# Five rearrangements in a two-layer token model on one core: row-max split inside its pass, early region padding, a new order at the gate's end, ranks and projection moved, embedding by batches

## The chip, the cores and the metric

One core of a Trainium2 chip runs the whole program. Five engines work beside each other, each on its own list of instructions: PE (TensorE, matrix products), DVE (VectorE), ACT (ScalarE), POOL (GpSimd) and SP (SyncE, which only issues DMAs). They meet through semaphores. The metric is the device time of one execution in microseconds (us), the median of several.

## The reference

4096 tokens (8 sequences of 512, width 192) pass five blocks, each added to the stream `h`:

```python
tok = wte[input_ids]                                   # gathered rows
Q, V = ln(tok) @ W_proj.T, tok @ W_val.T               # 8 heads of 64
trace = 0.99 * trace0 + 0.1 * einsum('bhip,bhiq->hpq', Q[:, :, :-2], V[:, :, 2:]) / denom
h  = shifted(Q) @ trace, heads joined, @ W_out.T       # L0 token block
h += linear_attention(layernorm(h))                    # 12 heads of 16, 44 features
h += soft_moe(layernorm(h))                            # 64 experts
h += attention_with_fake_quant(layernorm(h))           # 12 heads, 8 bits
x  = h_norm + attention(layer_norm(h_norm))            # full softmax, float32 accuracy
h += x + moe_mlp(layer_norm(x))                        # top 2 of 8 experts, hidden 768
```

In the last line each token goes to its two best experts by `xn @ gate_w`, and the two results are added with softmax weights.

## The kernel before

The program is six stages, each one or more blocks; all engines meet at a block's end. A batch is one sequence: 128 partitions by T = 4 tokens by 192. `Fori` is a loop on the engine itself; a Python loop is written out. `Link` makes DVE wait for its own last instruction; `Signal` is a semaphore that is counted per batch.

**Embedding, `embed_and_trace` (0 to 146 us).** POOL gathers the token rows by 32 indirect DMAs (line 246), four a batch, and waits for batch b-1 to land before it issues batch b+1. DVE and PE wait for all seven weight loads first. DVE computes the statistics of four batches together (`stats(half)`, L266, L151 to L156, L273) and then in a loop normalises each (`rows(b, j)`: four L279, L283, L284). PE (`products`) shifts rows (L361), turns them (L368) and adds their products with later rows (L375); ACT copies (L327, L331). After the last batch come small products one after the other: L388, L395, L400, then L406 (8 heads of 64 rows), and then h itself (L419), for which ACT first copies each batch of QT to a staging tile QTs (L348).

**Quantised attention, `quantised_attention`.** Its first pass over the scores (PE L1651, DVE L1661, ACT L1685) is a loop over batches. SP's part of it only spreads the queries of a batch over partitions (L1636, 4 DMAs), when the batch two before is done.

**Routed attention, `routed_attention` (from 1598 us).** A preparing block loads weights, and on POOL sets `Wp` to 0 (L2006), the ones of `V` (L2007) and the ones rows of the two key stacks (L2010); DVE waits for all. Pass 1 computes all scores in bf16 parts (PE L2202) and DVE keeps each row's maximum in `MX` (L2072); between score units, PE makes the queries, keys and values of batch b+2. The next block is pass 2. It begins by splitting `MX` into three bf16 parts on DVE (L2426, L2428), turning them (PE L2283), copying them (DVE L2431, ACT L2397), and placing them into rows of the query stack by DMA (L2251, `shift_rows`), so that the product gives score minus maximum. Then for each batch there are 12 steps n: PE makes the next two score pairs (L2296), ACT takes their exp (L2410), PE multiplies by values (L2360). PE runs ahead by one step. In the steps of batch b it also works for earlier ones: at n = 1 `ranks(b - 2)` (L2331, L2333), then `project(b - 1)` half 0 (L2309), at n = 3 half 1, at n = 8, 9, 11 the turned rows (L2315) and gate logits (L2323) of b-1. DVE divides the output (L2511 to L2517, result `OT`), finds the best two experts (`best_two`, to L2480), prepares the next residual rows (L2499, L2501), adds the projection (L2442; in `add_projection` preceded by `places`, L2486 to L2494), takes statistics and normalises (L2459). POOL computes rstd (L2558), scales (L2562, L2565) and sends the rows to their experts' regions in `routed_in` by indirect DMA (`send`, L2574), two sends of 4 DMAs a batch; the second waits until the first has landed, because both read one buffer whose return index is rewritten between them.

After the last batch DVE works out which tile belongs to which expert (up to `m.TID`, L2547), and SP then pads each expert's region behind its last row (L2269, 8 DMAs of 196 KB at places read from a table) and loads the first four experts' weights (L2593, 1252 KB each).

**Routed experts, `routed_experts`.** The block loads row tiles (SP L2620, L2621), after the pads have landed, turns them (PE L2654) and runs 39 tiles of two products (L2664, L2668, L2679). A last block adds the returned rows.

Of the kernel before, what the change touches and what calls it, by code (L numbers as in the profile page):

```python
# [9 lines left out]
BF16 = mybir.dt.bfloat16  # L10
# [148 lines left out]
def setup(nc, m, io):  # L159
# [19 lines left out]
    m.zero_filled = nc.alloc_semaphore("zero_filled")  # L179


def embed_and_trace(nc, m, io):
# [8 lines left out]
    QTs = [e(DC, [NC, T, P + 1]) for _ in range(2)]  # L191
    w = Cut(m.arena, R_AT + 4 * SLOT, E_AT)
    WpT, WvT = w(DC, [NC, TH * TD]), w(DC, [NC, TH * TD])
    WoT, Wp = w(TD, [TH, D]), w(TD, [TH, D])
    tr0, trT = w(TD, [TH, TD]), w(TD, [TH, TD])
    YT, U = w(DC, [NC, TH * TD]), w(TD, [TH, D])
# [6 lines left out]
    s_idx, s_w, s_const, s_rows, s_tok = sem("idx_loaded"), sem("tok_weights_loaded"), sem("constants_set"), \  # L203
        [nc.alloc_semaphore(f"rows_gathered{b}") for b in range(B)], sem("tok_ready")
# [7 lines left out]
    s_lk, s_qs, s_h, s_hc, s_l3, s_sk = (sem(n) for n in (  # L212
        "embed_chain", "q_staged", "h_product", "h_stored", "embed_chain3", "embed_stats_chain"))
    NH2 = B * T // 2

    with nc.Block(no_gpsimd_drain=True) as block:
        @block.sync
        def _(sp):
            sp.dma_start(idx, io.x.rearrange("b (p t) -> p b t", t=T)).then_inc(s_idx, 16)
            for dst, src in ((lnw, io.tok_ln_w.partition_broadcast(P)), (lnb, io.tok_ln_b.partition_broadcast(P)),  # L220
                             (WpT, io.tok_WpT.rearrange("(c p) n -> p c n", c=NC)),
                             (WvT, io.tok_WvT.rearrange("(c p) n -> p c n", c=NC)),
                             (WoT, io.tok_WoT.rearrange("(h p) n -> p h n", h=TH)),
                             (Wp, io.tok_W_proj.rearrange("(h p) n -> p h n", h=TH)),
                             (tr0, io.tok_trace0T.rearrange("h q p -> q h p"))):
                sp.dma_start(dst, src).then_inc(s_w, 16)

        @block.gpsimd
        def _(pool):
# [14 lines left out]
            for b in range(B):  # L244
# [7 lines left out]
            pool.wait_ge(s_rows[B - 1], 16 * T)  # L252
            pool.sem_inc(s_tok, 1)

        @block.vector
        def _(v):
            v.memset(QT[:, :, :, :, 0], 0.0)
            v.wait_ge(s_w, 16 * 7)

            def stats(half):  # L260

                link = Link(v, s_sk, 8 * half)
                for b in range(B // 2 * half, B // 2 * (half + 1)):
                    v.wait_ge(s_tok, b + 1)
                    for t in range(T):
                        ins = v.bn_stats(m.ST[:, b, t, :], tok[:, b, t, :])  # L266
                link(ins)
                part = lambda a: a.rearrange("p b t -> p (b t)")[:, NH2 * half:NH2 * (half + 1)]
                ln_constants(v, link, m.ST.rearrange("p b t k -> p (b t) k")[:, NH2 * half:NH2 * (half + 1), :],
                             part(m.wk[0]), part(m.wk[1]), part(m.mean), part(m.var))  # L270
                v.sem_inc(s_v, 1)
                v.wait_ge(s_std, half + 1)
                link(v.reciprocal(part(m.rstd), part(m.wk[2])))  # L273

            def rows(b, j):

                v.wait_ge(s_tsfree, b + 1)
# [17 lines left out]
            v.tensor_copy(YT, ps[0:DC, 0:2, :]).then_inc(s_yc, 1)  # L295
            v.tensor_scalar(tr0, tr0, 0.99, None, ALU.mult).then_inc(s_l3, 1)
# [6 lines left out]
            v.tensor_copy(U.rearrange("p (k h) n -> p k h n", k=4),  # L303
                          ps[0:TD, 4:8, 0:2 * D].rearrange("p k (h n) -> p k h n", h=2)).then_inc(s_gc, 1)
# [14 lines left out]
        def _(act):  # L319
# [3 lines left out]
            def part(b, j):  # L323
# [10 lines left out]
            for half in range(2):  # L334
# [2506 lines left out]
```

## Time and profile before

| | us |
|---|---|
| median of 3 runs | 2666.76 (2664.4 to 2668.61) |
| the profiled execution | 2661.37 |
| its span, first to last instruction | 2659.7 |
| busy in it: PE, DVE, ACT, POOL | 1947.6, 1493.0, 1065.1, 395.2 |

The span is what the rows below count from. Busy time of an engine says little alone: the stages follow each other and have different limits. Rows of the timeline give start, duration, engine, source line, operation, written tile, read tile, shape and count; in brackets, how long the engine had been idle and what released it. PEld is PE's weight load, SPq and ACTq are issues of DMAs. All tiles lie in one SBUF tensor, so they are called `arena`; `ps` is PSUM.

### The profile page before, as it was taken

The numbers are of one execution on the slowest core, as the hardware profiler recorded it, in microseconds if no ns is written. First come the engines' busy times: TensorE is split into PE (matmuls) and PEld (weight loads), VectorE is DVE, ScalarE is ACT, GpSimd is POOL, SyncE is SP. The second block draws the span as 40 slices with busy tenths as digits, with TensorE's granted clock in tenths as the row PEclk, the third lists the DMA queues.
The fourth block names the chain that finished last, engine by engine and source line by source line (L and its number), as shares of the span: only waits on it lengthen the run. The fifth ranks groups of instructions, "written<-read, shape, count | busy, mean of one in ns | idle before, by whom it ended". The sixth has DMA issues, their size and how long they took to land. (4 is left out here: it accounts for less than half of the span.)

```text
span 2659.7 us, 31420 instructions
## 1 busy us (share of the span) xinstructions
PE 1947.6 (73%) x9554; PEld 1023.9 (38%) x9576; DVE 1493.0 (56%) x2473; ACT 1065.1 (40%) x1846; POOL 395.2 (15%) x551
## 2 busy tenths in 40 slices
PE   3868878857876341777478854888798885699994
PEld 2645644435334120000111122333133332588884
DVE  3358348854002665999667772888957675011113
ACT  1100312223111256999678852222076663122221
POOL 5000000000111000212100004222003334122221
PEclk9889989967787565555589976777598997799997
DMA  3011110031994000000000004777676741565664
GB/s 76 0 35 30 48 30 24 10 154 61 365 411 164 12 0 16 12 12 12 27 20 30 24 0 84 112 108 103 70 84 87 91 55 40 197 206 196 206 211 177
DMA packets 130459, 239.43 MB, mean 90 GB/s; under 512 B 28618, under 2 KB 98475, under 8 KB 125228
## 3 DMA queue, kind: packets, MB, share of 16 engines
q1 hardware_dynamic: 118716, 216.85, 32.2%
q0 software_dynamic: 10480, 18.04, 2.1%
q10 hardware_dynamic: 1152, 3.15, 0.3%
q8 instruction: 60, 0.98, 0.2%
q14 instruction: 51, 0.42, 0.1%
HBM read 196.16 MB, written 32.02 MB: 86 GB/s over the span
## 5 line engine op out<-in xcount | busy, mean ns | idle before, releaser
L1651 PE MATMUL ps<-arena 128*128 x376 | 192.6, 615 | 125.3 <-ACT ps L1685 62.7
L1685 ACT ACTIVATE ps<-ps,arena 128x512 f32<-128x512 f32 x384 | 257.0, 1454 | 8.0 <-POOL arena L1671 8.0
L1661 DVE TENSOR_REDUCE arena<-ps 128x1024 f32 x192 | 234.8, 1226 | 38.0 <-PE ps L1651 22.1
L2072 DVE TENSOR_REDUCE arena<-ps 128x1024 f32 x192 | 227.3, 1222 | 49.7 <-PE ps L2202 43.0
L1685 ACT ACTIVATION_READ_ACCUMULATOR ps<-ps,arena 128x1 f32 x384 | 239.8, 1001 | 0.0
L2410 ACT ACTIVATE arena<-ps 128x1024 f32<-128x1024 f32 x192 | 185.2, 1022 | 78.9 <-PE ps L2296 73.5
L1835 ACT ACTIVATE arena<-ps 128x1024 f32<-128x1024 f32 x192 | 187.5, 1024 | 33.8 <-DVE arena L1857 29.1
L2202 PE MATMUL ps<-arena 96*128 96x512 bf16 x384 | 159.1, 508 | 41.3 <-DVE arena L2072 28.0
L2703 ACT ACTIVATE arena<-ps,arena 128x256 f32<-128x256 f32 x234 | 89.7, 482 | 235.8 <-PE ps L2668 229.9
L2723 DVE TENSOR_TENSOR arena<-ps,arena 128x384 f32<-128x384 f32 x39 | 21.8, 558 | 286.5 <-PE ps L2679 286.5
L538 PE MATMUL ps<-arena 96*128 96x456 f32 (+1 forms) x512 | 171.5, 488 | 9.6 <-DMA arena<-arena 6.0
L1857 DVE TENSOR_SCALAR arena<-arena 128x1024 bf16<-128x1024 f32 x192 | 130.9, 692 | 68.8 <-ACT arena L1835 67.2
L2679 PE MATMUL ps<-arena 128*128 128x192 f32 x936 | 162.5, 330 | 0.7 <-DVE arena L2723 0.7
L2679 PEld LDWEIGHTS ps<-arena 128*128 128x128 f32 x936 | 151.0, 190 | 13.6 <-issue 13.6
L1651 PEld LDWEIGHTS ps<-arena 128*128 128x128 bf16 x384 | 25.6, 110 | 291.6 <-ACT ps L1685 197.8
L1795 PE MATMUL ps<-arena 128*128 (+1 forms) x370 | 116.1, 394 | 17.7 <-DMA arena<-arena 15.2
L538 PEld LDWEIGHTS ps<-arena 96*128 96x128 f32 x512 | 97.8, 199 | 74.0 <-issue 56.2
L2638 POOL DMA_INDIRECT routed_out<-arena x78 | 75.7, 971 | 288.2 <-DVE arena L2723 275.5
L2664 PE MATMUL ps<-arena 128*128 128x256 f32 x468 | 109.2, 384 | 0.9 <-DVE arena L2717 0.9
L1813 PE MATMUL ps<-arena 128*32 128x512 bf16 x384 | 76.7, 396 | 40.7 <-DVE arena L1857 33.7
L2360 PE MATMUL ps<-arena 128*32 128x512 f32 x768 | 104.7, 618 | 0.9 <-ACT arena L2410 0.9
L2296 PE MATMUL ps<-arena 99*128 99x512 bf16 x384 | 103.2, 393 | 2.6 <-DMA arena<-arena 2.6
(379 smaller groups left out, 3219.6 us busy)
## 6 DMA issues: line engine op xcount, KB each, us to landing
arena<-in_sm_w_dram SPq DMA_DIRECT2D x128, 576.0 KB
arena<-in_re_w_dram SPq DMA_DIRECT2D x39, 1252.0 KB, 6.0
arena<-ra_parts SPq DMA_DIRECT2D x192, 192.0 KB, 9.8
ra_parts<-arena SPq DMA_DIRECT2D x48, 192.0 KB, 2.5
arena<-routed_in SPq DMA_DIRECT2D x39, 196.0 KB, 5.4
arena<-la_xt SPq DMA_DIRECT2D x16, 384.0 KB, 3.4
arena<-arena SPq DMA_DIRECT2D x64, 96.0 KB, 2.2
arena<-routed_out SPq DMA_DIRECT2D x16, 384.0 KB, 8.7
```

The lines of the kernel that those rows point to most:

```text
L538: ins = pe.matmul(ps[:, 2 * (t % 2) + bank, to:to + w], XTs[j][:, c, t * P:(t + 1) * P], Wx[:, kind, c, at:at + w], start=(c == 0), stop=( ...
L1651: ins = pe.matmul(ps[:, 2 * (n % 4) + t % 2, :], QM[j][:, h, t * P:(t + 1) * P], KI[:, b, h // HG, :], start=True, stop=True)
L1661: v.tensor_reduce(MXq[:, b, 2 * u:2 * u + 2, at_head(h)], ps[:, 2 * (n % 4):2 * (n % 4) + 2, :], AX.X, ALU.max).then_inc(s_lk, 1)
L1685: ins = act.activation(bank, bank, ACT.Exp, bias=nb[n % 4][:, t % 2:t % 2 + 1], scale=c_reg, accum_out=RS[:, b, t, at_head(h):at_head(h) + 1])
L1795: ins = pe.matmul(ps[:, 2 * (n % 3) + q, :], QM[j][:, h, c * P:(c + 1) * P], QI[:, bass.ds(b, 1), g, :].rearrange("p o s -> p (o s)"), sta ...
L1835: act.activation(PF[n % 2], ps[:, 2 * (n % 3):2 * (n % 3) + 2, :].rearrange("p a s -> p (a s)"), ACT.Exp, scale=c_reg).then_inc(pe_.sem, 1)
L1857: v.tensor_scalar(PB[n % 2], PF[n % 2], MAGIC, MAGIC, ALU.add, ALU.subtract).then_inc(rd.sem, 1)
L2072: v.tensor_reduce(MX[:, bass.ds(b, 1), 2 * (n % 2):2 * (n % 2) + 2, n // 2].rearrange("p o t -> p (o t)"), ps[:, 2 * (n % 2):2 * (n % 2) + ...
L2202: ins = pe.matmul(ps[:, t, :], ST_[j][0][0:KR, h, t * P:(t + 1) * P], ST_[j][1][0:KR, h, :], start=True, stop=True)
L2410: act.activation(PF[e // 2 % 2][:, 2 * (e % 2):2 * (e % 2) + 2, :], ps[:, 2 * (e % 3):2 * (e % 3) + 2, :], ACT.Exp, scale=HD ** -0.5).then ...
L2664: pe.matmul(unit(k), wr[:, k * P:(k + 1) * P], XT[j][:, 0, :], start=True, stop=False)
L2679: ins = pe.matmul(ps[:, 7, h * D:(h + 1) * D], HT[j][:, k, h * P:(h + 1) * P], wr[:, at:at + D], start=(k == 0), stop=(k == KH - 1))
```

## The change

- Embedding: no loops on the engines; POOL issues all 32 gathers without waiting; the two layer norm rows have their own semaphore, and the other weights are waited for only where they are used; DVE's statistics go batch by batch, those of b+1 ahead of the rows of b; ACT's square root likewise; L406's product takes two heads (128 rows) at a time, so 8 products instead of 16; QTs and its copies are gone.
- Regions: SP fills every region of `routed_in` with the pad rows (17 tiles of 256 rows for each of 8 experts) during the first pass of the quantised attention, one DMA a batch. POOL waits for these before its first send. The 8 late pads are gone.
- Preparing block of the routed attention: only `Wp` is set; the ones are set by POOL in pass 1, after the splitting of the first two batches.
- Row-max split: POOL splits batches 0 to 5 within pass 1; PE turns them in pass 1's batch 6, two transposes a score unit, ACT copies them, then loads the exp table; SP places batches 0 and 1. Batches 6 and 7 are split by POOL at the start of pass 2, while PE has issued the first two score pairs, and PE waits for them before the third.
- Pass 2: `ranks(b - 2)` from n = 1 to n = 3, projection halves from n = 1 and 3 to n = 2 and 3; `read_ranks` (two reads of PSUM) between the two additions, the rest of `places` after them; the addition to `m.H` from after `norm` to ahead of the logits' copy.
- Gate's end: half 0 of the last projection ahead of `ranks(B - 2)`, half 1 in another bank and without waiting for the first addition; the last batch's second send reads a copy of the rows, made by POOL, and so does not wait for the first to land; SP loads weights 0 and 1, then rows 0 and 1 as soon as all sends have landed, then weights 2 and 3, all ahead of the block's end.

The diff's core:

```diff
@@ embed_and_trace
-                if b:
-                    pool.wait_ge(s_rows[b - 1], 16 * T)
-                    pool.sem_inc(s_tok, 1)
-            for half in range(2):
-                stats(half)
-                with v.Fori(B // 4 * half, B // 4 * (half + 1)) as i:
-                    rows(2 * i, 0)
-                    rows(2 * i + 1, 1)
+            stats(0)
+            for b in range(B):
+                if b + 1 < B:
+                    stats(b + 1)
+                rows(b)
@@ quantised_attention, first pass, SP
+                    sp.dma_start(io.routed_in[bass.ds(b * region, region)].rearrange("(n r) d -> n (r d)", r=TR),
+                                 pad_rows[None, :].to_broadcast([PART, TR * RW])).then_inc(m.padded, 16)
@@ routed_attention
+    def split_maxima(pool, b):
+        rows = slice(b * T, (b + 1) * T)
+        for k in range(3):
+            pool.tensor_copy(BP[:, rows, k, :], M[:, rows, :]).then_inc(s_c, 1)
+            pool.wait_ge(s_c, 5 * b + 2 * k + 1)
+            if k < 2:
+                pool.tensor_tensor(M[:, rows, :], M[:, rows, :], BP[:, rows, k, :], ALU.subtract).then_inc(s_c, 1)
+                pool.wait_ge(s_c, 5 * b + 2 * k + 2)
...
+            for b in range(2, B):
+                split(b)
+                mx.wait(pool, b - 2, NU)
+                split_maxima(pool, b - 2)
@@ pass 2, PE
-                    if b > 1 and n == 1:
+                    if b > 1 and n == 3:
+                        xx.wait(pe, b - 1, 1)
                         ranks(b - 2, 7 - j)
-                    if behind and n in (1, 3):
-                        project(b - 1, 1 - j, n // 2)
+                    if behind and n in (2, 3):
+                        project(b - 1, 7 - j, n - 2)
...
+            pe.wait_ge(s_c, 5 * B)
+            for k in range(2 * T):
+                ins = turn_parts(pe, AHEAD + k // T, k % T, 7)
...
-            ranks(B - 2, 7)
-            project(B - 1, 1, 0)
-            project(B - 1, 1, 1)
             ex.wait(pe, B - 1, 2 * NS)
+            project(B - 1, 7, 0)
+            ranks(B - 2, 5)
+            project(B - 1, 3, 1)
@@ pass 2, SP
-            for n in range(NX):
-                at = sp.value_load(m.PADS[0:1, n:n + 1], min_val=0, max_val=NX * PART * TR - TR)
-                sp.dma_start(xd[bass.ds(at, TR)], xd[NX * PART * TR:(NX * PART + 1) * TR]).then_inc(m.padded, 16)
-                if n % 2 == 0:
-                    load_weights(sp, io, m, n // 2)
+            load_weights(sp, io, m, 0)
+            load_weights(sp, io, m, 1)
+            at = [tile_at(sp, m, n) for n in range(2)]
+            for k in range(2):
+                sp.wait_ge(s_sc[k], 16 * T * B)
+            for n in range(2):
+                load_rows(sp, io, m, n, at[n])
+            load_weights(sp, io, m, 2)
+            load_weights(sp, io, m, 3)
```

## Rows read from the trace of the kernel before

**Rows 1.** Sums by stretch: from:to, length, then each engine's busy time.

```profile
960.00:1240.00 280.00, 160.18 (x354) 26.27 (x360) 222.97 (x202) 241.40 (x622) 45.23 (x148) 0.53 0.05 12
...
1931.40:2218.00 286.60, 252.62 (x1501) 101.61 (x1499) 201.53 (x431) 193.74 (x206) 83.46 (x81) 0.94 0.57 76
...
2256.50:2282.30 25.80, 0.00 (x0) 0.00 (x0) 0.07 (x1) 0.00 (x0) 4.16 (x6) 0.50 0.77 291
```

**Rows 2.** Timeline of the embedding's first part.

```profile
16.89 1.14 DVE L266 BATCH_NORM_STATS2 arena<-arena 128x6 f32<-128x192 f32 x4 [15.85 <-DMA arena<-in_tok_trace0T_dram]
...
32.10 1.25 DVE L279 TENSOR_SCALAR arena<-arena 128x192 f32 x4 [0.53 <-DVE arena L273]
...
41.15 0.96 DVE L284 TENSOR_TENSOR arena<-arena 128x768 f32<-128x768 f32 x1 [1.12 <-issue]
...
46.99 0.95 POOL L246 DMA_INDIRECT arena<-in_tok_wte_dram,arena  x1 [0.30 <-issue]
51.10 0.49 ACT L327 ACTIVATE arena<-ps 128x384 f32<-128x384 f32 x1 [11.94 <-remote]
...
92.25 0.65 PEld L383 LDWEIGHTS ps<-arena 128*96 128x96 f32 x4
```

**Rows 3.** Timeline of its second part.

```profile
106.90 10.55 PE L406 MATMUL ps<-arena 64*96 64x192 f32 x32 [1.84 <-DVE arena L303]
...
118.26 2.02 ACT L348 ACTIVATE arena<-arena 96x1032 f32 x2 [27.56 <-PEq L410]
```

**Rows 4.** Timeline of the routed attention's preparing block.

```profile
1599.46 4.53 DVE L156 TENSOR_SCALAR arena<-arena 128x32 f32<-128x32 f32 x1
...
1604.02 10.37 POOL L2010 MEMSET arena<- 3x6144 bf16 x2
...
1614.62 0.48 DVE L2026 MEMSET arena<- 1x512 f32 x1 [7.07 <-POOL arena L2010]
```

**Rows 5.** Timeline between pass 1 and pass 2.

```profile
1921.77 0.36 DVE L2426 CAST arena<-arena 128x384 bf16<-128x384 f32 x1 [0.67 <-PEq L2054]
...
1924.16 3.60 PE L2283 MATMUL ps<-arena 128*36 128x128 bf16 x32 [4.43 <-DVE arena L2426]
...
1931.37 2.85 ACT L2410 ACTIVATE arena<-ps 128x1024 f32<-128x1024 f32 x3 [0.41 <-PE ps L2296]
```

**Rows 6.** Timeline of pass 2, batch 7's first steps.

```profile
2187.42 0.69 DVE L2517 TENSOR_TENSOR arena<-arena 128x512 f32<-128x512 f32 x1
...
2189.99 3.66 PE L2309 MATMUL ps<-arena 128*128 128x192 f32 x12
2191.35 0.96 DVE L2501 TENSOR_TENSOR arena<-arena 128x768 f32<-128x768 f32 x1
...
2194.12 3.90 ACT L2410 ACTIVATE arena<-ps 128x1024 f32<-128x1024 f32 x4 [7.42 <-PE ps L2296]
...
2197.40 2.22 PE L2309 MATMUL ps<-arena 128*128 128x192 f32 x12
...
2200.09 1.02 ACT L2410 ACTIVATE arena<-ps 128x1024 f32<-128x1024 f32 x1 [2.07 <-PE ps L2296]
```

**Rows 7.** Timeline from the end of pass 2 to the first expert tile.

```profile
2233.24 1.01 POOL L2574 DMA_INDIRECT routed_in<-arena  x1 [14.83 <-DVE arena L2494]
...
2239.47 1.25 DVE L2459 TENSOR_SCALAR arena<-arena 128x192 f32<-128x192 f32 x4 [1.16 <-POOL arena L2558]
...
2255.18 0.18 DVE L2547 TENSOR_SCALAR arena<-arena 128x39 int32<-128x39 f32 x1
...
2258.97 0.98 POOL L2574 DMA_INDIRECT routed_in<-arena  x1 [0.64 <-POOL arena L2569]
...
2278.72 0.69 SPq L2620 DMA_DIRECT2D arena<-routed_in  x1
...
2282.31 1.12 PE L2654 MATMUL ps<-arena 128*128 128x128 f32 x4 [32.57 <-DMA arena<-routed_in]
```

**Rows 8.** The page's group of the quantised pass's maxima.

```profile
L1661 DVE TENSOR_REDUCE arena<-ps 128x1024 f32 x192 | 234.8, 1226 | 38.0 <-PE ps L1651 22.1
```

More of the change, by code:

```diff
@@ L179, in setup @@
     m.zero_filled = nc.alloc_semaphore("zero_filled")
+    m.padded = nc.alloc_semaphore("re_pads_stored")
+    m.xm = [nc.alloc_semaphore(f"re_rows_loaded{j}") for j in range(2)]
 def embed_and_trace(nc, m, io):
@@ L321, in _, with std, part @@
             act.sem_inc(s_qtc, 1)
-            def part(b, j):
+            def std(b):
+                act.wait_ge(s_v, b + 1)
+                act.activation(m.wk[2][:, b, :], m.var[:, b, :], ACT.Sqrt, bias=m.eps, scale=1.0 / D
+                               ).then_inc(s_std, 1)
+            def part(b):
+                j = b % 2
                 act.wait_ge(s_shift, b + 1)
@@ L332, in part @@
                                    ACT.Copy).then_inc(s_qtc, 1)
-            for half in range(2):
-                some = lambda a: a.rearrange("p b t -> p (b t)")[:, NH2 * half:NH2 * (half + 1)]
-                act.wait_ge(s_v, half + 1)
-                act.activation(some(m.wk[2]), some(m.var), ACT.Sqrt, bias=m.eps, scale=1.0 / D).then_inc(s_std, 1)
-                with act.Fori(B // 4 * half, B // 4 * (half + 1)) as i:
-                    part(2 * i, 0)
-                    part(2 * i + 1, 1)
-            act.wait_ge(s_qtc, 2 * B + 1)
-            with act.Fori(0, B // 2) as i:
-                for j in range(2):
-                    b = 2 * i + j
-                    act.wait_ge(s_h, b + 1)
-                    act.activation(QTs[j], QT[:, :, b, :, :], ACT.Copy).then_inc(s_qs, 1)
+            std(0)
+            for b in range(B):
+                if b + 1 < B:
+                    std(b + 1)
+                part(b)
         @block.tensor
@@ L377, in products @@
                 ins.then_inc(s_tsfree, 1)
-            with pe.Fori(0, B // 2) as i:
-                products(2 * i, 0)
-                products(2 * i + 1, 1)
+            for b in range(B):
+                products(b, b % 2)
             for c in range(NC):
@@ L384, in _ @@
             ins.then_inc(s_cp, 1)
+            pe.wait_ge(s_w, 16 * 5)
             pe.wait_ge(s_c, 1)
@@ L410, in _ @@
             pe.sem_inc(s_h, 2)
-            with pe.Fori(0, B // 2) as i:
+            pe.wait_ge(s_qtc, 2 * B + 1)
+            for i in range(B // 2):
                 for j in range(2):
                     b = 2 * i + j
-                    pe.wait_ge(s_qs, b + 1)
                     pe.wait_ge(s_hc, b + 1)
@@ L2114, in _ @@
                 ins.then_inc(vd.sem, 1)
+            for u in range(AHEAD // 2):
+                act.wait_ge(s_bt, u + 1)
+                act.activation(*turned_parts(u, 4 + u), ACT.Copy).then_inc(s_bc, 1)
+            act.activation(spare, m.one, ACT.Exp)
         @block.gpsimd
@@ L2119, in _, with split @@
             p2.start(pool)
-            with pool.Fori(0, B) as b:
+            def split(b):
                 for k in range(2):
@@ L2141, in _ @@
             pool.wait_ge(s_gw, 80)
+            with pool.Fori(0, 2) as b:
+                split(b)
+            pool.memset(V.rearrange("p b (n k d) -> p (b n) k d", k=2, d=HD)[:, :, 1, :], 1.0).then_inc(s_z, 1)
+            for j in range(2):
+                pool.wait_ge(s_z, 2 + j)
+                pool.memset(ST_[j][1][KR:KR + 3, :, :], 1.0).then_inc(s_z, 1)
+            for b in range(2, B):
+                split(b)
+                mx.wait(pool, b - 2, NU)
+                split_maxima(pool, b - 2)
+            pool.wait_ge(s_z, 4)
         @block.sync
@@ L2390, in _ @@
             logits(B - 1, 4)
+            po.wait(pe, B - 2, 1)
             ranks(B - 1, 5)
```

237 lines of the change are left out of this document (123 added, 114 removed).

## Prediction

> **What bounds the kernel now.** I read the page, then the sums by stretch, the waits, and the timeline at each place that the diff touches. No engine bounds the whole: each stage has its own chain, so an edit is worth what its own stretch gives. The reader is to see five places.
>
> The embedding's first part ends at 92.25, after a start at 16.89, and holds a hole: ACT sat idle for 11.94 until 51.10 while POOL issued the last gathers (the last at 46.99) [rows 2]. Its second part is a chain of small products, the longest 10.55 [rows 3]. The preparing block ends when POOL's last memset lets DVE go on at 1614.62, after 7.07 of idle [rows 4]. Between pass 1 and pass 2, DVE starts splitting at 1921.77 and the first exp starts at 1931.37 [rows 5]. In pass 2 ACT is the nearest to a bound but is busy only 193.7 of 286.6 us; PE 252.6 [rows 1]. In batch 7 it waits 7.42 and then 2.07 for scores that PE can't issue, because PE stands in a projection or before one [rows 6]. The same pair of gaps stands in batches 2 to 6. The gate's end runs from the last sends to the first expert tile at 2282.31; PE had been idle for 32.57 [rows 7], and DMA moved 291 GB/s there, four weights of 1252 KB and the pads [rows 1]. The tile loop behind it (39 tiles, PE-bound) is untouched and only shifts.
>
> **The sum, part by part.**
>
> *Embedding, first part.* DVE now needs for a batch: statistics 1.14 and six tiny operations of about 0.2, so 2.4, and rows 1.25 + 2 x 0.96 and a reciprocal with its waits, about 3.9 [rows 2]; 6.3 in all, more than PE's products (5.1 a batch in the same timeline, by estimate from its steady batches). Eight batches from 16.89 end at 67.5, and the last products 5.1 later, at 72.6: a gain of 19.6. Against it stands what gathers do to DVE. From 32.10 to 42.11, when the add that starts at 41.15 ends, DVE did two batches of rows, 6.3 of work in 10.0: 3.7 lost, with an idle of 1.12 before the last [rows 2]. All of it fell on the second batch. Now some two to three batches of rows lie beside gathers: 8 to 11 lost, gain 8.6 to 12. The hole is the other bound: if DVE and ACT again stand still until the gathers have landed, some 46, six to seven batches remain and the gain is nil (-1). What the hole is, no row says: its releaser is "remote" [rows 2]. The loops' branch and register instructions fall in it, which now are gone; POOL's gathers fall in it too. I take 11, nearest to the measured loss, with -1 and 19.6 as ends.
>
> A rule of the Trainium skill speaks against this part: "SBUF — State Buffer", section "SBUF: two separate sides", says that GpSimd and a two-port VectorE operation share a port pair as an exclusive lock, and the loser waits for the whole instruction. The 4.53 of L156 under a POOL memset, a 128x32 operation, is of that kind [rows 4]. By it each of a batch's four scaled rows could wait out one gather issue of 0.95; that is 3.8 a batch, the same as the loss measured, so the sum by it is that of the 8 to 11 above.
>
> *Embedding, second part.* L406 took 10.55 for 32 records [rows 3]; with 16 it takes half, 5.3 gained. PE no longer waits for ACT's first staging copy, one of the two that take 2.02 [rows 3]: 1.1. Together 6.4. Bounds 5 and 8 (the copy of its input is over half as many elements too).
>
> *Preparing block.* DVE was ready at 1607.55 (1614.62 - 7.07), and even that was late by some 4.3, since L156 took 4.53 instead of the 0.2 of its like [rows 4]. The memsets gone, the weights bound it: at the least 7.07 is gained, at the most 11.3. The loads were issued beside the memset and I have no landing for the last; I take 7.5. The memsets (about 5, by what L156 waited, and 10.37 [rows 4]) go to POOL after the second batch's split. In pass 1 POOL has 17 us free there before the third batch, 15.6 are needed; if the cover fails, 1 to 2 us of the third batch's split come late, and that has a whole batch of slack. Cost taken 0.
>
> *Pass 1.* 24 transposes at 3.60 / 32 = 0.11 [rows 5], two a score unit: 0.22 beside DVE maxima of 1.22, on a PE that takes 1.04 of it. Cost 0 to 1.5, taken 0.5. POOL's splits wait for the maxima with nothing urgent queued behind. ACT's copies and table load come while it is idle.
>
> *Between the passes.* The first two exps start about 1 us into pass 2. Then PE waits for POOL: ten dependent operations on 128x48 elements. POOL has no such row; its operations go from 0.27 for next to nothing to 1.8 for 128x768, so 0.2 to 0.3 each and as much again for the wait on the last: 3 to 5.5, then eight transposes, 0.9, and 1 to the exp. The third exp comes at 1921.8 + 5 to 7.5 instead of 1931.37 + 2: a gain of 4 to 6.5, taken 5. Batch 1's key stack loads start 9 us earlier.
>
> *Pass 2.* I redo batch 7's start by rows 6. `OT` is ready at 2188.11. Before, PE waited for `mk` too (best_two, 1.5 more), then ran half 0 cold in 3.66, and ACT began again at 2194.12; half 1 began at 2197.40 and the exp after it at 2200.09. Now PE has done step 2's scores meanwhile, starts half 0 at 2188.15, warm like the other half, 2.22; scores of step 3 to 2191.4, values to 2192.5; DVE ends L2501 at 2192.31 and adds half 0 to 2192.9, so PE waits 0.4; ranks 0.15 and half 1 2.22, to 2195.3; next exp at 2196.0 instead of 2200.09. That is 4.1. `places` behind the second addition puts DVE 0.8 later and the move of the 0.95 addition to `m.H` puts it earlier again: 0.3 at the turned rows' wait. So 4.4 for each of six batches, and 3.5 for batch 1, which has no ranks: 30. DVE's chain is then as long as before within a period of 33 and has 201.5 of work in 286.6 [rows 1], so it doesn't become the bound. If half 0 stays cold (3.66), each batch gains 1.4 less: 20. I take 29, bounds 19 and 33.
>
> *Gate's end.* Half 0 starts with `OT`, 1.7 earlier, so places and the sends of batch 6 come 1.4 earlier; POOL's four issues (from 2233.24, 1.28 apart) still stand before rstd, so norm at 2239.47 comes 1.3 earlier, and the tables too: 2253.9 instead of 2255.36 [rows 7]. The last send began at 2258.97, after the landing of the one before; it now needs only its index rows: 2257.6 less some 1.7, so its four issues run from 2255.9 to 2260.8 and land at 2262.4 (1.6 as with the earlier one). POOL's added copy of 128x768 has its cover in the wait for the tables' chain. SP issues weights 0 and 1 at 2255 to 2256.6, rows at 2262.5. Before, rows were issued at 2278.72 and PE started at 2282.31, 3.6 later [rows 7]. So rows land at 2266.1; SP still issues weights 2 and 3, to 2268, and the block's end adds 1: PE starts at 2269.1. Gain 13.2, taken 13. At 291 GB/s [rows 1] weights 0 and 1 (2.56 MB) take 8.8, so rows wait for at most 1 to 3 of it: bounds 10 and 15.
>
> *Pads.* 17 x 256 rows x 784 B = 3.41 MB a batch, 27.3 MB in all, where DMA was busy 0.05 at 12 GB/s [rows 1]. At 291 GB/s one takes 11.7 of a batch's 32; the spreads for the next batch are issued a batch ahead. Cost 0 to 3 (first batch), taken 0.5. Old pads: in the gate's end.
>
> Sum: 11 + 6.4 + 7.5 - 0.5 + 5 + 29 + 13 - 0.5 = 70.9. The profiled execution takes 2661.37 and would take 2590.5; it stands 5.4 under the median, so the median goes to 2596.
>
> **Rivals.** *The gathers hold the embedding.* For: the hole, and the lock. Against: its loop instructions are gone. Gain 11 falls to -1: 2608. *Pass 2's wait only moves*: PE then waits at step 3 for DVE's first addition, and half 0 stays cold. For: the addition ends only after L2501, and PE is given little to do before it. Against: the 0.4 worked out. Gain 29 falls to 14: 2611. *The pads make the quantised pass slower*, the one on the other side: nothing in the trace moves data from DRAM to DRAM alone, at whole regions. The pass lasts some 260 (its maxima alone are busy 234.8 and idle 38.0 [rows 8]). Below 27.3 MB / 260 us = 105 GB/s the spreads queue behind pads; from 83 GB/s on (330 us) all 71 are lost and the kernel is slower; at 70 it is 2720. Against: 291 GB/s with such pads in the mix. *The change does little*: each seam freed is closed again by a DMA (weights, stacks), and only pass 2's gain is left: 2638.
>
> **Chances.** Forecast 0.72 (own range 2576 to 2604), gathers 0.10, moved wait 0.08, both of these together 0.03 (2623), pads 0.03, little 0.04. The range 2574 to 2618 leaves about 0.15 out. Within 0.2% (about what a measurement of this kernel can tell from no change) is 2661.4 to 2672.1: 0.02; slower 0.03; faster 0.95.
>
> **What would show it.** Right: L383 near 81; L406 with 16 records near 5.3; DVE's L2026 counterpart near 7 us after the block's start instead of 16; one short gap, about 2, then 3 in ACT's exps of each batch where 7.42 and 2.07 stood, a period of 33.2 instead of 37.6; between last maximum and third exp 6 to 8; PE's idle before the first tile 19 instead of 32.57. Wrong: a hole in DVE until the last gather has landed; POOL's split over 6; a "DMA" releaser before L1651 in later batches; a first tile that waits for weights.

## The result, and the profile after

The changed kernel takes 3332.24 us (median of 4 runs, 3330.79 to 3333.27) against 2666.15: a ratio of 1.2497, 95% interval [1.2475, 1.2519]. Forecast were 2596 and a range of 2574 to 2618. The step that had 0.5 us in the sum cost 735. The others together gave 65.7 of the 71.4 forecast for them, single ones missing by up to 6 either way. Times of other runs are compared with the kernel before on the same chip, which takes about 2665 us on some chips and 2655 on others.

The page's groups of the quantised attention and its DMA rows, of the changed kernel:

```profile
L1646 PE MATMUL ps<-arena 128*128 x376 | 186.3, 607 | 796.7 <-DMA arena<-arena 738.6
L1656 DVE TENSOR_REDUCE arena<-ps 128x1024 f32 x192 | 231.3, 1224 | 706.6 <-PE ps L1646 694.3
...
arena<-arena SPq DMA_DIRECT2D x64, 96.0 KB, 11.7
```

The maxima are as busy as before, 231.3 us, but DVE is idle for 706.6 ahead of them where [rows 8] has 38.0. PE waited 738.6 for a copy from `arena` to `arena`: the spreads of the queries (L1629). The waits give total, number and longest:

```profile
PE ps L1646 <- DMA arena<-arena: 738.6, 8, 98.4
```

Eight waits, one for each batch. The first, of 62.6, stands in the kernel before as well, where it is the only one; the other seven last 96.0 to 98.4 and make the 676 that are new. SP's timeline for one batch:

```profile
1199.44 14.63 SPq L1631 DMA_DIRECT2D routed_in<-routed_in  x1
1214.38 109.81 SPq L1629 DMA_DIRECT2D arena<-arena  x4
1324.39 14.63 SPq L1631 DMA_DIRECT2D routed_in<-routed_in  x1
```

From pad to pad it is 124.95 us, and SP stands for 109.81 of it over four spreads, behind the pad: their issues take 68.97, 11.11, 14.66 and 14.65, where 0.63 to 0.66 is usual. Meanwhile the DMA engines are all but idle, as the DMA view of 1200 to 1330 shows (each digit is a fortieth of the stretch; the last figure is the share of sixteen engines' time):

```profile
DMA  1000000000000000000000000100010001000010
...
DMA packets 608, 3.95 MB, mean 30 GB/s; under 512 B 80, under 2 KB 537, under 8 KB 537
...
q1 hardware_dynamic: 606, 3.93, 7.6%
```

One pad is 3332 KB (3.41 MB); in 124.95 us that is 27.3 GB/s. 7.6% of sixteen engines is 1.2 engines. So the pass isn't short of DMA engines: the pad keeps about one of them busy and the small copies are held up behind it.

### The profile page after: what moved, and what is told of

Read it like the earlier page. It is cut to its first block and busy times, and to the rows that moved or that the text cites. A ratio compares the mean times of both kernels' runs of the same rounds, so it can differ in the third digit from the quotient of the medians.

```text
span 3328.8 us, 31172 instructions
## 1 busy us (share of the span) xinstructions
PE 1922.7 (58%) x9538; PEld 1008.8 (30%) x9560; DVE 1503.1 (45%) x2508; ACT 1059.0 (32%) x1847; POOL 405.1 (12%) x592
## 5 line engine op out<-in xcount | busy, mean ns | idle before, releaser
L1646 PE MATMUL ps<-arena 128*128 x376 | 186.3, 607 | 796.7 <-DMA arena<-arena 738.6
L1656 DVE TENSOR_REDUCE arena<-ps 128x1024 f32 x192 | 231.3, 1224 | 706.6 <-PE ps L1646 694.3
L1666 POOL TENSOR_SCALAR arena<-arena 128x2 f32<-128x2 f32 x192 | 51.0, 266 | 920.4 <-DVE arena L1656 919.5
L1680 ACT ACTIVATION_READ_ACCUMULATOR ps<-ps,arena 128x1 f32 x384 | 134.1, 349 | 0.0
## 6 DMA issues: line engine op xcount, KB each, us to landing
arena<-arena SPq DMA_DIRECT2D x64, 96.0 KB, 11.7
```

The costliest lines, as they stand in the source:

```text
L1646: ins = pe.matmul(ps[:, 2 * (n % 4) + t % 2, :], QM[j][:, h, t * P:(t + 1) * P], KI[:, b, h // HG, :], start=True, stop=True)
L1656: v.tensor_reduce(MXq[:, b, 2 * u:2 * u + 2, at_head(h)], ps[:, 2 * (n % 4):2 * (n % 4) + 2, :], AX.X, ALU.max).then_inc(s_lk, 1)
L1680: ins = act.activation(bank, bank, ACT.Exp, bias=nb[n % 4][:, t % 2:t % 2 + 1], scale=c_reg, accum_out=RS[:, b, t, at_head(h):at_head(h) + 1])
```

## The experiments

**1. The pads' shape.** The changed kernel writes a pad as 17 tiles of 196 KB, the tiles outermost. Three runs change only how the same bytes are described, and a fourth puts the late pads back.

```diff
@@ changed kernel; its copies are [17 tiles][196 KB]
-  dst = region.rearrange("(n r) d -> n (r d)", r=TR); src = pad_rows[None, :].to_broadcast([PART, TR * RW])
@@ pads_16_outer (K = 16), pads_4_outer (K = 4): [K pieces][17 tiles]
+  dst = region.rearrange("(n k r) d -> k n (r d)", k=K, n=PART); src = pad_rows in K pieces, broadcast over n inside
@@ pads_tiles_outer: [17 tiles][16 pieces]
+  dst = region.rearrange("(n k r) d -> n k (r d)", k=16, n=PART)
@@ pads_late: no early pads, no wait of POOL for them; behind the tables, on SP
+  for n in range(NX): at = value_load(m.PADS[n]); dma_start(xd[at:at + TR], pad tile)   # weights 0 and 1 among them, rows 0 and 1 behind them
```

> The changed kernel, with each early pad DMA (3332 KB) cut into pieces of 12.5 KB in place of 50 KB, 17 tiles still outermost (17 x 16 x 12.5 KB). In the changed kernel one such pad took 125 us: 27 GB/s, and the loads of spread queries behind it landed with it. Theory A, the outermost size 17 keeps the copy on one DMA engine: nothing changes, 3332 us. Theory B, copying from DRAM to DRAM out of one 196 KB source is slow in any form: 3332 us as well. Theory C, the long pieces are what is slow: about 2600 us.

> The changed kernel, with the same bytes of each early pad DMA described with 16 pieces of a tile outermost and the 17 tiles inside (16 x 17 x 12.5 KB). Theory A: sixteen engines share it, 125 / 16 = 8 us a pad, hidden in a batch's 32; the kernel gains what its other parts gained by the two traces, 735 - 669 = 66 us: 2600 us. Theory B (source or DRAM bound): 3332 us. Theory C (long pieces): about 2600 us too. With the run where 17 is outermost, A and C part. The Trainium skill, page 'DMA: Bandwidth & Descriptors', section 'Why a DMA increments its semaphore by 16 and not by 1', states theory A: a copy uses as many engines, up to 16, as divide the outermost sizes of both sides, so 17 gives one and 16 gives sixteen.

> The same with four pieces of a tile outermost (4 x 17 x 50 KB, pieces as long as in the changed kernel). Theory A: four engines, 125 / 4 = 31 us a pad, just under a batch's 32: 2600 to 2625 us, and GB/s about 108 while a pad runs. Theory B: 3332 us. Theory C: 3332 us, since the pieces are as long as before. A count of engines that doesn't scale would give a time in between.

> The changed kernel with the regions padded late as in the kernel before: eight DMAs of 196 KB behind the tables, and rows of the first tiles loaded behind them; all other parts of the change stay. All theories: the other parts' gain, 66 us, less what the late pads cost at the end of the gate, 2 to 6 us (eight issues of about 0.7 and the rows behind them): 2602 to 2607 us. If the other parts gained nothing the time would be 2666; then the 66 us would have come from the slow pass itself.

| run | us | ratio to before, interval |
|---|---|---|
| pads_tiles_outer | 3331.38 (1 run) | |
| pads_16_outer | 2597.27 | 0.9751 [0.9737, 0.9764] |
| pads_4_outer | 2602.89 | 0.9767 [0.9752, 0.9782] |
| pads_late | 2605.13 | 0.9773 [0.976, 0.9786] |

With 16 pieces outermost a pad lands in 13.8 us (the page's row; 3.41 MB / 13.8 = 247 GB/s), and the spreads in 2.2:

```profile
routed_in<-routed_in SPq DMA_DIRECT2D x8, 3332.0 KB, 13.8
...
arena<-arena SPq DMA_DIRECT2D x64, 96.0 KB, 2.2
```

The same bytes from the same source at 247 GB/s: theory B (DRAM or the single source) falls. With four pieces outermost, in the stretch of one pad:

```profile
DMA packets 208, 3.15 MB, mean 107 GB/s; under 512 B 28, under 2 KB 146, under 8 KB 146
```

107 GB/s is four times 27, as forecast, and the pieces were 50 KB (62 packets over 8 KB for 3.1 MB), as long as in the changed kernel: theory C (long pieces) falls with it. pads_tiles_outer tells less than it was meant to: its 16 pieces of a tile lie behind each other, the copy that was issued had the 50 KB pieces of the changed kernel again (18 packets and 0.90 MB in a stretch), and so it was the same copy. What decides is the size of the outermost dimension: 17 gave 27 GB/s, 4 gave 107, 16 gave 247. The queue's rows tell how many engines worked, as packets, MB and share of sixteen engines' time; pads_tiles_outer (1098 to 1131), pads_4_outer (1100.9 to 1130.2) and pads_16_outer (1096 to 1106), each within a pad:

```profile
q1 hardware_dynamic: 18, 0.90, 6.3%
...
q1 hardware_dynamic: 206, 3.13, 25.5%
...
q1 hardware_dynamic: 235, 2.95, 97.0%
```

One sixteenth is 6.25%, so these are one engine, four and nearly all. The "8 us a pad" of theory A was too short by 6: from four engines to sixteen the rate grew 2.3 times, not 4; why is open. The Trainium skill, "DMA: Bandwidth & Descriptors", section "Why a DMA increments its semaphore by 16 and not by 1", states the rule: a copy runs on the largest number of engines, up to 16, that divides the outermost sizes of both its sides. By that rule 17, a prime, gets one; these runs agree.

The quantised pass, from its first product to the next block's, took 270.40 us with the pads well shaped (1028.50 to 1298.90), and 270.8 without them in the kernel before. The two windows:

```profile
1045.80:1316.60 270.80, 192.61 (x376) 25.48 (x383) 239.01 (x202) 259.05 (x770) 51.78 (x193) 0.51 0.06 16
```

```profile
1028.50:1298.90 270.40, 193.58 (x376) 25.54 (x383) 238.98 (x202) 258.69 (x770) 51.30 (x193) 0.51 0.37 117
```

DMA's share goes from 0.06 to 0.37, and no engine's busy time moves. So the cover that the prediction counted on was there, for a pad that takes 13.8 us and not for one of 125.

**2. The same copy from another queue.** The one-engine copy was left as it is and issued by POOL.

```diff
-                    sp.dma_start(region b, pad_rows broadcast over 17 tiles).then_inc(m.padded, 16)
+                pool.dma_start(region b, pad_rows broadcast over 17 tiles).then_inc(m.padded, 16)   # ahead of batch b's 24 operations
```

> The changed kernel (3332 us), its early pads as they are there (17 tiles outermost), but issued from POOL's queue instead of SP's, so that the loads of spread queries don't stand behind them in the same queue. Theory A, one DMA engine works through a pad either way, and the 738 us were the spreads standing behind it in SP's queue: the quantised pass takes its 270 us again, the pads go on beside the later stages for 8 x 125 = 1000 us until about 2030, and POOL's first send, near 1960, waits for them: 2600 to 2680 us. Theory B, whoever shares that one engine waits for the pads, whichever queue: the loads still take 20 us or more each and the kernel stays above 2800 us. A third way: POOL's queue shares the copy out over all engines by itself, then a pad takes some 8 us and the time is 2597.

It took 2761.56 us (1 run), between theories A and B. The DMA view of 1068 to 1300:

```profile
GB/s 26 26 35 29 58 84 53 53 52 52 52 52 40 48 93 54 53 54 52 120 79 79 79 79 79 79 96 65 52 129 79 79 79 80 119 120 93 88 79 89
```

The rate stands at 26, then 53, then 79: pads that were issued a batch apart run beside each other, each at the rate of one engine (POOL's queue holds 6.3% of sixteen engines, then 12.1% and 18.2%, in 1070 to 1094, 1110 to 1140 and 1190 to 1230). SP's don't: with two pads issued, the changed kernel's queue holds 6.4% (1080 to 1140). The Trainium skill, same page and section, states that POOL's copies take their engines in turn where SP's take the lowest-numbered; that fits the steps. The spreads still came late: PE waited 212.5 us for them in six waits. The first was 114.4 instead of the usual 62.6, and four later ones took 22.0 to 25.8 each. SP issues nearly all spreads in 0.63 us again, but all four of a batch are seen landed only 42.6 to 55.2 us after the last issue, once 103.6, where 2.2 is usual. So leaving SP's queue took most of the loss away and not all, and the rest lies behind the issue; that it is a share of the same engines was not measured by itself.

**3. Pass 2's order alone.** 16 pieces outermost, and the order of ranks, projection and `places` as before.

```diff
-                    if b > 1 and n == 3:
-                        xx.wait(pe, b - 1, 1)
+                    if b > 1 and n == 1:
                         ranks(b - 2, 7 - j)
-                    if behind and n in (2, 3):
-                        project(b - 1, 7 - j, n - 2)
+                    if behind and n in (1, 3):
+                        project(b - 1, 7 - j, n // 2)
@@ add_projection: read_ranks and places together, ahead of the first addition
```

> The run with 16 pieces outermost (2597.3 us), with the order of pass 2 as in the kernel before: ranks at step 1, projection halves at steps 1 and 3, places ahead of the first addition. All else of the change stays. The prediction's step says 29 us for this order (19 to 33): 2626 us, and the gaps of 7.42 and 2.07 before the exps come back. Rival: what shortened the batches from 37.7 to 33.5 us is the addition to m.H moved off the way, or the ones and stacks prepared earlier; then most of it stays: 2597 to 2605 us.

2603.44 us where the kernel before took 2654.43: ratio 0.9811 [0.9796, 0.9826]. (This group, and the last one, ran on a chip where the kernel before takes some 10 us less. The 2603.44 lies within the rival's 2597 to 2605 for that reason alone.) weights_2_3_later, a run of the same group that has the new order and otherwise differs by a weight load, took 2579.53 (0.9714): 23.9 less, and 20.2 less by the spans of the two traces. ACT's exps of batch 7, first with the old order, then in the changed kernel:

```profile
2141.67 3.90 ACT L2443 ACTIVATE arena<-ps 128x1024 f32<-128x1024 f32 x4 [8.31 <-PE ps L2326]
2147.65 2.99 ACT L2443 ACTIVATE arena<-ps 128x1024 f32<-128x1024 f32 x3 [2.07 <-PE ps L2326]
```

```profile
2871.98 1.94 ACT L2443 ACTIVATE arena<-ps 128x1024 f32<-128x1024 f32 x2 [2.19 <-PE ps L2325]
2876.88 1.94 ACT L2443 ACTIVATE arena<-ps 128x1024 f32<-128x1024 f32 x2 [2.96 <-PE ps L2325]
```

The old pair of gaps of [rows 6] is back in pass2_old_order (8.31 and 2.07 for 7.42 and 2.07); the new order has 2.19 and 2.96, forecast as "about 2, then 3". From third to last exp the old order takes 281.0 us, the new one 254.3 to 261.0 in thirteen: 20 to 27 us hang on the order (23 to 27 within the group). The move of the addition to `m.H` stayed in, so it isn't part of this. The rival (most of it stays) falls.

**4. The gate's end.** The changed kernel, from the last batch's best two to the first tile:

```profile
2923.84 1.80 POOL L2598 TENSOR_TENSOR arena<-arena 128x768 f32<-128x768 f32 x1
...
2924.15 1.52 DVE L2505 CAST arena<-arena 128x8 f32<-128x8 uint32 x1
...
2938.23 0.96 POOL L2610 DMA_INDIRECT routed_in<-arena  x1 [0.30 <-issue]
2944.32 0.72 SPq L2640 DMA_DIRECT2D arena<-routed_in  x1
...
2951.49 1.09 PE L2704 MATMUL ps<-arena 128*128 128x128 f32 x4 [24.41 <-DVEq L137]
```

From the last exp to this tile it is 57.6 us, 65.4 before: 7.9 gained of 13. Three places differ from the forecast. A CAST of 128x8 takes 1.52 and ends at 2925.67, with POOL's addition at 2925.64. SP sees the sends landed 5.1 after the last issue's end (2939.19 to 2944.32), not 1.7. And rows reach PE 7.2 after their issue, not 6.6. Each got a run; the first two in the order in which they add up, the third with the weights of tiles 2 and 3 alone moved.

```diff
@@ scale_before_sends, POOL
+                if p == B - 2:
+                    scale(p + 1)          # ahead of the wait and send(p, 1), not behind them
@@ gate_end_reordered, SP, on top of it
             load_weights(sp, io, m, 0)
-            load_weights(sp, io, m, 1)
             ... wait for the sends, load rows 0 and 1 ...
-            load_weights(sp, io, m, 2)
-            load_weights(sp, io, m, 3)
+            load_weights(sp, io, m, 1)   # 2 and 3 in the next block; this alone is weights_2_3_later
```

> The run with 16 pieces outermost (2597.3 us), with the loads of the third and fourth expert's weights issued after the block's end, in the next block, instead of ahead of it. In the changed kernel PE's first turned rows were released by the block's end at 2951.49, while the rows had been issued from 2944.32 to 2947.30 and SP's two weight issues ran from 2947.34 to 2949.6. Theory A, SP's own list holds the block's end: PE starts 2 us earlier and the third tile's weights are not waited for: 2595.3 us. Theory B, the rows' landing (2.8 us after their issue, as in the tile loop) is what PE would wait for next: 1 us or less. Theory C, the weights come late for tile 3: no gain or 1 to 3 us slower.

> The run with 16 pieces outermost once more, so that the two behind it and the kernel before are compared on one chip. Ratio 0.9751 as measured before, [0.973, 0.977]; if the chip is one without ACT's stop 0.970 to 0.976, since both kernels lose their stop but the shares of it differ by a few us.

> The run with 16 pieces outermost, with POOL's scaling of the last batch's rows put ahead of the second send of batch 6. In the changed kernel the CAST of best_two took 1.52 us (0.17 to 0.31 before) and ended with POOL's 1.80 us addition, and the next product 0.70, ending with POOL's copy; tables came at 30.0 us after OT where 29.7 stood before and 28.3 was predicted. Theory A, DVE stood behind POOL's operations there: the CAST falls to about 0.2, the tables come 1.7 us earlier, the sends stay (POOL has the same work), and of the 1.7 only the earlier weights are left: 0 to 2 us faster. Theory B, the CAST is slow by itself or by the scatter's DMA: no change of the CAST. Later sends would show as a loss of up to 2 us. The Trainium skill, page 'SBUF — State Buffer', section 'SBUF: two separate sides', states theory A's mechanism: GpSimd and some VectorE operations lock a shared port against each other for a whole instruction.

> The same, and SP loads only the first expert's weights ahead of the rows of tiles 0 and 1, the second's behind them, the third's and fourth's in the next block. In the changed kernel the last sends were seen landed 4.94 us after their last issue's end, against the 1.6 predicted, with two weights (2.5 MB) issued 5.4 us before; rows issued at 2944.32 reached PE at 2951.49. Theory A, the two weights held the sends: landing takes 1.6 to 3, and with 2 us from the weights behind the block's end the kernel gains 4 to 7 us over the run with 16 pieces: 0.973 of the kernel before or less. Theory B, the landing has its own length: only 2 us are gained. Theory C: PE then waits for the second weights, and 0 to 2 are left.

| run | us | ratio to before, interval |
|---|---|---|
| weights_2_3_later (chip with 2654.43 before) | 2579.53 | 0.9714 [0.9698, 0.973] |
| pads_16_again | 2596.75 | 0.975 [0.9736, 0.9765] |
| scale_before_sends | 2596.91 | 0.974 [0.9726, 0.9753] |
| gate_end_reordered | 2594.92 | 0.9737 [0.9723, 0.975] |

The times can't tell the last three apart; the traces can. In scale_before_sends the CAST:

```profile
2195.32 0.17 DVE L2506 CAST arena<-arena 128x8 f32<-128x8 uint32 x1
```

0.17 for 1.52: with POOL's operation elsewhere DVE doesn't stand, and the tables come 28.6 after `OT` (28.3 forecast, 30.0 in pads_16_again). But the last send ends 0.9 later (36.5 after `OT` there, 37.4 here), since POOL now scales ahead of batch 6's second send, so next to nothing is gained at the first tile (57.2 from the last exp for 57.4). The Trainium skill, "SBUF — State Buffer", section "SBUF: two separate sides", says that GpSimd and some VectorE operations lock a shared port pair against each other for a whole instruction; the trace agrees with it here. In gate_end_reordered, with one weight ahead of the rows:

```profile
2202.77 0.97 POOL L2609 DMA_INDIRECT routed_in<-arena  x1 [0.30 <-issue]
2205.34 0.72 SPq L2642 DMA_DIRECT2D arena<-routed_in  x1
...
2211.43 1.09 PE L2708 MATMUL ps<-arena 128*128 128x128 f32 x4 [22.57 <-DVEq L137]
```

1.6 from last issue's end to rows, where scale_before_sends, with two weights ahead of them, has 3.9 and pads_16_again 5.0: the second weight had held the sends. From pass 2's last product to this tile it is 52.8 us, 56.3 in pads_16_again, so 3.5 earlier, of which 2.1 are left at the first tile's last products (2226.76 for 2228.81). Moving weights 2 and 3 alone gave 1.9 in the trace (54.44 for 56.39 in pads_16_outer, of another chip; rows to PE 5.3 for 7.2), as its theory A said; no time on one chip compares the two. The 4 to 7 expected of the whole were too much. It is the fastest measured where before takes 2665, but 1.8 us don't set it apart from pads_16_again.

**5. The embedding's first part.**

```diff
             for b in range(B):
+                if b == B // 2:
+                    pool.wait_ge(s_ts, 2)     # gathers_paused; both_reordered has it and the gate's end of 4
                 for t in range(T): ... gather ...
```

> The run with 16 pieces outermost (2597.3 us), and POOL stops after the gathers of four batches until ACT has made its shifted copy of batch 1. In the changed kernel ACT stood still for 14.47 us before that copy, until 48.56, with its input ready at 33.25, and DVE for 3.59 until 47.75; the last gather was issued at 43.14, and the DMA engines fell silent at 46. In the kernel before the same copy came at 51.10, its last gather at 46.99. Theory A, the stop lasts until gathers are out of the way: now the queue is empty by about 32, ACT goes on at 34 to 36, and the first part ends 8 to 12 us earlier, less what sixteen gathers beside it cost DVE: 2586 to 2592 us. Theory B, the stop is one of DVE and POOL in turn at their memory port, and the gathers' issue time is lost wherever it lies: 2595 to 2599 us, no change. Theory C, ACT's stop is code that arrives late and has nothing to do with gathers: ACT's copy stays near 48, 2597 us or slower, since the gathers of the later batches come late.

> The kernel before, unchanged, profiled on the chip of this group. In the last group the kernel before ran at 2654.4 us where it had run at 2665.2, and the variants' first part of the embedding ended at 69.1 to 69.4 us where it had ended at 84.4 to 86.2, without ACT's stop of 14 us. Theory A, the stop belongs to the chip and not to the change: on a chip where the kernel takes some 2654 the kernel before has no stop of 11.94 either, its first part ends near 81, and the new first part gains 12 there against 6 to 8 on the first chip. Theory B, only the changed code can escape the stop (no loops): the kernel before stops here too, ends near 92, and the change gains over 20 in the first part on such a chip.

> The run with the gathers held back after four batches, once more. Where it first ran, the other kernels of its group showed no stop of ACT at batch 1, so the pause could not remove one: the first part ended at 73.2 us with the pause and at 69.1 to 69.4 without. In the other groups the stop stood in the kernel before (twice, until 51) and in seven changed ones (until 48.6 in one read closely; first part at 84.4 to 86.2). If this chip shows the stop (the kernel before at about 2665 us): Theory A, the stop lasts until gathers are out of the way: ACT copies batch 1 by 36, the first part ends near 73 to 78, ratio 0.970 to 0.972 of the kernel before, where the unpaused one has 0.975. Theory C, code that arrives late whatever POOL does: ACT's copy stays near 48, the pause lasts as long, the later gathers come late: ratio 0.976 or more. If the chip doesn't show it (about 2654 us): 0.973 as before, and the question stays open.

> The run with the end of the gate reordered (0.9737 of the kernel before), with the same pause. Theory A on a chip with the stop: another 8 to 12 us, 0.969 to 0.971. Theory C, or no stop: 0.973 to 0.976. It shows, beside the other run, whether the gain is the same in a second kernel.

gathers_paused 0.9733 [0.9719, 0.9746], gathers_paused_again 0.9737 [0.972, 0.9754], both_reordered 0.9712 [0.9698, 0.9725], the last two with 2656.34 before; before_again 2666.98 us (1 run). both_reordered is below the 0.973 to 0.976 expected without a stop; its gate's end is 3.7 us shorter than that of gathers_paused_again (53.9 for 57.7), and the rest of their 8 us isn't placed. In the kernel before, read again where it takes 2665, and in weights_2_3_later, ACT's shifted copy of batch 1:

```profile
50.99 0.49 ACT L327 ACTIVATE arena<-ps 128x384 f32<-128x384 f32 x1 [11.59 <-remote]
```

```profile
31.62 0.49 ACT L328 ACTIVATE arena<-ps 128x384 f32<-128x384 f32 x1 [3.47 <-PE ps L351]
...
69.36 0.81 PE L372 MATMUL ps<-arena 128*96 128x192 f32 x4
```

On the chips with 2665, both profiles of the kernel before have the stop, until 51, and all eight changed ones, until 48.1 to 48.8 whenever it began (11.7 to 19.9 long). On those with 2654 and 2656 none of six has it: their first part ends at 69.1 to 69.4, with the pause at 72.1 to 73.4, instead of 84.4 to 86.2. So for the changed kernels the stop goes with the chip that a group ran on, not with their differences. Whether the kernel before has it on the other chips isn't shown, since both its profiles are from chips with 2665. What it is stays open: no chip that shows it ran the pause. The gathers alone don't make it, since weights_2_3_later issues all 32 without waiting, until 44.6, and has none. Where it is absent the pause only costs, some 4 us.

## Why the prediction was wrong, step by step

pads_16_outer, which differs in the pads' shape alone, takes 2597.27 us, next to the 2596 forecast. That it is so near is luck: 6 too little for one step and 3 and 5 too much for two others partly cancel, and its profiled execution, at 2596.02 where 2590.5 was forecast, happens to lie 1.3 under the median and not 5.4. Its trace gives each step its size. It spans 2594.0 where before's spans 2659.7: 65.7 gained, of 70.9 forecast.

| step | forecast | measured | from |
|---|---|---|---|
| pads (changed kernel) | -0.5 | -735 | 665 in the first pass, 70 more before the second |
| embedding, first part | +11 | +8.0 | product of L372 at 84.40, of L383 at 92.42 |
| embedding, second part | +6.4 | +12.5 | to the next block's product: 62.1 to 49.6 |
| preparing block | +7.5 | +7.4 | first product of L1930 to the first transpose: 53.1 to 45.7 |
| pass 1 | -0.5 | -2.0 | first transpose to last score: 302.8 to 304.8 |
| between the passes | +5 | +6.5 | last maximum to third exp: 12.1 to 5.6 |
| pass 2 | +29 | +28.1 | third to last exp: 283.7 to 255.6 |
| gate's end | +13 | +7.9 | last exp to first tile |
| stages not touched | 0 | -2.8 | they vary by 5 between two profiles of one kernel |

**Pads: the step that failed.** "At 291 GB/s one takes 11.7 of a batch's 32." The rate was that of four weights and eight small pads together [rows 1], copies of 128 rows and of one contiguous tile; this one had 17 tiles outermost. It took 125 us, and the spreads "issued a batch ahead" stood behind it in SP's queue: the rate was wrong, and with it the overlap. The rival had the mechanism, a rate below 105 GB/s, and its scale: 27.3 MB at 27.3 GB/s make 1000 us, 730 over the pass's 270. It got 0.03 because 291 GB/s spoke against it, a rate of other copies. The shape, which the diff shows, had not been costed.

**First part.** The number was near and the reason wrong. The 8 to 11 were to be lost by DVE beside gathers. In weights_2_3_later all gathers lie beside DVE too, and it loses nothing:

```profile
24.33 1.13 DVE L261 BATCH_NORM_STATS2 arena<-arena 128x6 f32<-128x192 f32 x4
...
27.09 1.30 DVE L274 TENSOR_SCALAR arena<-arena 128x192 f32<-128x192 f32 x4
...
30.28 1.13 DVE L261 BATCH_NORM_STATS2 arena<-arena 128x6 f32<-128x192 f32 x4
```

The last of them is issued at 43.68. A batch takes 5.95, less than the 6.3 worked out without any loss, and the four scaled rows 1.30: the 3.8 a batch that the prediction works out for the port lock isn't there. The part ends at 69.4, before the 72.6 of the bound. On the chips with 2665 it is the stop that takes the time (19.92 in pads_16_outer, 14.47 in the changed kernel, 11.94 before). That is the hole of the rival, and with it the part still gained 8.0, not the rival's -1. So the loss of 3.7 that the prediction read from [rows 2] is more likely a piece of it than the gathers' doing; that isn't shown by a run.

**Second part.** The term was too small because it left steps out. Before and in pads_16_outer:

```profile
92.90:143.00 50.10, 43.46 (x219) 37.41 (x217) 19.77 (x41) 8.41 (x8) 0.00 (x0) 0.80 0.00 0
...
119.38 23.57 PE L419 MATMUL ps<-arena 96*128 96x192 f32 x128 [1.93 <-ACT arena L348]
```

```profile
84.40:122.90 38.50, 33.61 (x205) 29.27 (x204) 18.98 (x41) 0.00 (x0) 0.00 (x0) 0.96 0.00 1
...
101.82 21.04 PE L409 MATMUL ps<-arena 96*128 96x192 f32 x128 [0.89 <-DVE arena L301]
```

The two terms of the sum came as forecast: 6.0 by the product (10.55 to 4.52, forecast 5.3) and 1.0 by the staging copy (1.1). The other 5.5 had no term. The product before it, with its copy, gained 2.5 (L400 3.26, L390 1.52; before_again has 2.82 with a granted clock of 1.00, so most of that isn't the clock). The loop of L419 gained 2.5 (23.57 to 21.04) and was never idle within, before or after, so this isn't the staging copies: before, its first 16 products come 0.32 apart, at a granted clock of 0.50 (1.2 GHz), and the others 0.16 at 1.00 (2.4 GHz), as all do in pads_16_outer. The last 0.5 lies behind the loop. The clock also moves L396 between profiles: 4.52 here, 2.84 in the changed kernel (granted 1.00 throughout), 5.44 in weights_2_3_later. PE had gaps of 0.7 to 1.9 between these products before and 0.7 to 1.3 in pads_16_outer; what kept the clock up is not shown. **Preparing block.** Right; DVE's start (2325.67 in the changed kernel) is now released by the landing of a weight, `in_ra_Wproj_dram`, after 3.97 of idle.

**Pass 1** cost 2.0, outside its 1.5. **Between the passes** POOL's ten operations took 3.1 us, 2634.37 to 2637.46, at 0.22 and 0.28 each with a tenth between them: the low end of the 3 to 5.5. **Pass 2** and its two gaps came as worked out: in batch 7 of the changed kernel half 0 starts 0.06 after `OT` and takes 2.22 at a granted clock of 1.00, where the 3.66 of [rows 6] ran at 0.59, PE waits 0.70 for DVE (0.4 forecast), and the exp comes 7.6 after `OT` (7.9). **Gate's end.** Three terms fell short, all in 4: DVE behind POOL's addition (1.5), which the prediction had not seen in DVE's way, the landing behind two weights (3.4; "rows wait for at most 1 to 3 of it" had weighed the rows and not the sends), and 0.6 from rows to PE.

The early pads, well shaped, are worth having: from last exp to first tile pads_late needs 63.9 us, pads_16_outer 57.5.

## What to carry to other kernels

Before giving a DMA a rate, read its outermost dimension on both sides: the same 3.41 MB took 125 us with 17 outermost, some 32 with 4 (at 107 GB/s), 13.8 with 16. A rate read from a mix of other transfers is no price for a copy of a new shape, and a slow background copy holds up the small, urgent copies that are issued behind it. When a chain is made earlier, look at what it now runs into: here a POOL operation and two weight loads took back 5 of 13 us, and moving the POOL operation gave none of it back, since it then stood ahead of a send.

## What the runs showed that was not expected

- The copy with 17 outermost keeps one of sixteen DMA engines busy (6.3%) and goes from DRAM to DRAM at 27 GB/s (3.41 MB in 124.95 us), and SP's issue of such a copy takes up to 14.63 us and of the spreads behind it 11 to 80 each, where 0.6 to 0.7 is usual.
- The same one-engine copies from POOL's queue add up, 26, 53, 79 GB/s, and two from SP's don't (28 GB/s).
- The same kernel differs by 10 us between chips (2665, 2655), and changed ones by 15 us in the first 90 us alone, by a stop of ACT that ends near 48.5 or isn't there.
- Beside 32 gathers issued without waiting DVE can run undisturbed: 5.95 us a batch where 6.3 were worked out without any loss.
